# Splat attention in a graph kernel: distances in five fp32r passes, scores over all 128 rows, normalisation per head, and transposes moved to the seams of groups

## What is computed

```python
qkv = (x @ qkv_w.T).reshape(b, t, 3, h, hd)
q, k, v = (qkv[:, :, 0], qkv[:, :, 1], qkv[:, :, 2])
centers = base_centers + center_deltas * ms
def splat_weights(tok):
    d2 = jnp.sum(tok ** 2, -1)[..., None] + c_sq[None, None] - 2.0 * jnp.einsum('bthd,hsd->bths', tok, centers)
    return jnp.exp(-d2 * inv_var[None, None]) * eff_amps[None, None]
qw = splat_weights(q)
kw = splat_weights(k)
logits = jnp.einsum('bihs,bjhs->bijh', qw, kw) / temp
attn = jax.nn.softmax(logits, axis=2)
out = jnp.einsum('bijh,bjhd->bihd', attn, v).reshape(b, t, d)
return out @ out_w.T
```

## Time and profile before

| | before |
|---|---|
| median of three executions | 940.78 us |
| the profiled execution, its own time | 937.67 us |
| its span, first to last instruction | 935.9 us |
| PE, DVE, ACT, POOL busy | 818.8, 602.2, 309.2, 61.4 us |
| chain that ended last, by engine | PE 17%, DVE 5%, ACT 1%, issue 1% of the span |

### The profile page before, as it was taken

The page is one execution under the profiler, slowest core; times in us unless marked ns, Lnnn a source line. Parts: engine busy times, 40 slices in busy tenths (PEclk is TensorE's granted clock), DMA queues, the critical chain, the costliest instruction groups (busy, mean ns, idle before and its releaser), DMA issues. The chain is left out here.

```text
span 935.9 us, 11276 instructions
## 1 busy us (share of the span) xinstructions
PE 818.8 (87%) x3978; PEld 563.4 (60%) x3978; DVE 602.2 (64%) x1180; ACT 309.2 (33%) x484; POOL 61.4 (7%) x60
## 2 busy tenths in 40 slices
PE   5788999999999960996769999988887999999788
PEld 3576788888778840332557778544454445546564
DVE  7646777776649553113882323688877888885876
ACT  2232334332214230112121103322313787884240
POOL 3000000000000004011280000000000000000010
PEclk9979999999999995999579999999998999999999
DMA  5814122210302415995320202000000100000002
GB/s 168 231 49 154 49 88 69 68 58 8 113 0 90 137 69 161 290 361 175 90 80 0 90 1 91 0 1 2 1 1 5 43 1 1 1 1 1 6 1 90
DMA packets 48150, 66.62 MB, mean 71 GB/s; under 512 B 4268, under 2 KB 22460, under 8 KB 48095
## 3 DMA queue, kind: packets, MB, share of 16 engines
q1 hardware_dynamic: 43903, 56.22, 18.8%
q0 software_dynamic: 2384, 6.92, 2.3%
q10 hardware_dynamic: 1808, 2.75, 0.8%
HBM read 56.38 MB, written 9.50 MB: 70 GB/s over the span
## 5 line engine op out<-in xcount | busy, mean ns | idle before, releaser
L851 PE MATMUL bank<-xT,slot 128*128 128x512 f32 (+1 forms) x248 | 105.3, 425 | 6.5 <-DVE xT L1564 5.7
L851 PE MATMUL bank<-slot 128*128 128x512 f32 (+1 forms) x212 | 87.7, 414 | 13.9 <-DVE slot L1566 8.3
L852 PE MATMUL bank<-xT,slot 128*128 128x512 f32 (+1 forms) x248 | 97.8, 394 | 0.0
L853 PE MATMUL bank<-xT,slot 128*128 128x512 f32 (+1 forms) x248 | 97.5, 393 | 0.0
L1314 ACT ACTIVATE slot<-bank 128x512 fp32r<-128x512 f32 (+3 forms) x60 | 33.9, 589 | 155.4 <-PE bank L1093 67.1
L2041 DVE TENSOR_REDUCE key<-bank 128x2 f32<-128x1024 f32 x64 | 75.3, 1218 | 14.8 <-PE bank L1153 14.8
L852 PE MATMUL bank<-slot 128*128 128x512 f32 (+1 forms) x212 | 84.2, 397 | 0.0
L853 PE MATMUL bank<-slot 128*128 128x512 f32 (+1 forms) x212 | 84.0, 396 | 0.0
L1501 ACT ACTIVATE arena<-bank 128x1024 f32<-128x1024 f32 x64 | 65.6, 1027 | 27.5 <-PE bank L1219 27.4
L851 PEld LDWEIGHTS bank<-xT,slot 128*128 128x128 f32 (+1 forms) x248 | 46.7, 188 | 22.5 <-issue 13.5
L1081 PE MATMUL bank<-arena,wraw 128*80 128x512 f32 x128 | 59.4, 609 | 0.0
(11 more groups left out here) (308 smaller groups left out, 1519.4 us busy)
## 6 DMA issues: line engine op xcount, KB each, us to landing
arena<-in_ewT SPq DMA_DIRECT2D x16, 1024.0 KB, 8.5
arena<-in_edge_attr SPq DMA_DIRECT2D x16, 512.0 KB, 3.9
wraw<-in_qkvT SPq DMA_DIRECT2D x3, 1024.0 KB, 5.2
expert_rows<-rows SPq DMA_DIRECT2D x1, 2560.0 KB, 13.6
wraw<-in_L_ffn_expert_b POOLq DMA_DIRECT2D x16, 160.0 KB, 5.8
expert_results<-wraw ACTq DMA_DIRECT2D x16, 160.0 KB, 5.7
xn<-in_x SPq DMA_DIRECT2D x4, 512.0 KB, 6.0
wraw<-in_L_mix_w_qkv SPq DMA_DIRECT2D x2, 1024.0 KB, 7.8
```

Source lines behind the costliest of these rows:

```text
L851: pe.matmul(out, L[1], R[0], start=start, stop=False, **kw)
L852: pe.matmul(out, L[0], R[0], start=False, stop=False, **kw)
L853: return pe.matmul(out, L[0], R[1], start=False, stop=stop, **kw)
```

## The change

- **Distances.** ACT's copy and square of a `p` go to `raw_sq`; ACT rounds both to a high half in one instruction over 1024 columns, and POOL subtracts for the low half (`split_sq`, a ring of four). `d2` becomes five fp32r passes: ones with the high and low squares, and `mm3` with the centres, which DVE splits once, after `cblk`. ACT also takes over the scaling and rounding of the weights.
- **Scores.** The keys of a pair are laid out twice with zeros in the other head's rows: POOL copies rows 0 to 63 of the key stack to `lone_keys` (second half of `wraw`) and clears them in the stack. `E` then takes 128 rows in both matmuls. For the unused rows to be harmless their log amplitude becomes -100.
- **Attention.** `normalise_group` becomes `normalise_head`, one head behind unit place 2 and the other behind place 3. `oT(g)` moves from place 4 of group g+1 to the seam of group g+2, between `E` and the first `O` (g = 0 to 4; 5, 6 and 7 stay late).
- **Staging.** `F` goes to the first staging buffer, behind the split of `Lo`.

```diff
+        if n >= lag and (n - lag) % T == 0 and n >= lag + 2 * T and (n - lag) // T - 2 != 2 * PAIRS - 3:
+            steps.append(("oT", (n - lag) // T - 2))
         if n >= lag:
             steps.append(("O", n - lag))
...
         if group > 0 and place == 2:
             steps.append(("oU", group - 1))
-        if group > 0 and place == 4 and group - 1 != 2 * PAIRS - 3:
+        if group > 0 and place == 3:
+            steps.append(("oN", group - 1))
+        if group == 2 * PAIRS - 1 and place == 4:
             steps.append(("oT", group - 1))
...
+            for i in range(4 * PAIRS):
+                pool.wait_ge(sq_hi, i + 1)
+                pool.tensor_tensor(split_sq[:, i % 4, 1], raw_sq[:, i % 4], f32(split_sq[:, i % 4, 0]), ALU.subtract).then_inc(sq_lo, 1)
+
+            pool.wait_ge(w_split, windex["Lv"] + 1)
+            pool.wait_ge(sq_lo, 4 * PAIRS)
+            pool.memset(f32(lone_keys)[64:128], 0.0).then_inc(keys_zeroed, 1)
+            pool.wait_ge(keys_zeroed, 1)
+            for c in range(PAIRS):
+                finished(pool, "L", c, T - 1, 1)
+                if c >= 2:
+                    finished(pool, "E", 2 * T * (c - 1) - 1)
+                both = slot[3][0:64, c // 2, 2 * (c % 2):2 * (c % 2) + 2, :].rearrange("p a i -> p (a i)")
+                pool.tensor_copy(lone_keys[0:64, c % 2, :], both.bitcast(F32)).then_inc(keys_copied, 1)
+                pool.wait_ge(keys_copied, c + 1)
+                pool.memset(both.bitcast(F32), 0.0).then_inc(keys_alone, 1)
...
-                    pe.matmul(o, onesblk, qsq[:, g % 2, 1, w], start=True, stop=False)
-                    close(pe.matmul(o, cblk[:, c, :], qsq[:, g % 2, 0, w], start=False, stop=True))
+                    pe.matmul(o, onesblk[:, :], split_sq[:, i % 4, 0, 1], start=True, stop=False)
+                    pe.matmul(o, onesblk[:, :], split_sq[:, i % 4, 1, 1], start=False, stop=False)
+                    close(mm3(o, [at_[:, c, :] for at_ in centers], [split_sq[:, i % 4, v, 0] for v in range(2)], False, True))
...
-                        r = krows(b, MROWS)
-                        ins = pe.matmul(bank[:, bank_of[step] + b, :], stack(3, c, r, jt * P, (jt + 1) * P),
-                                        stack(2, c, r, ih * HALF, (ih + 1) * HALF), start=True, stop=True)
+                    pe.wait_ge(keys_alone, c + 1)
+                    w, every = slice(jt * P, (jt + 1) * P), slice(0, P)
+                    for b, keys in enumerate((lone_keys[:, c % 2, w], stack(3, c, every, jt * P, (jt + 1) * P))):
+                        ins = pe.matmul(bank[:, bank_of[step] + b, :], keys,
+                                        stack(2, c, every, ih * HALF, (ih + 1) * HALF), start=True, stop=True)
...
+                    act.activation(raw_sq[:, i % 4, 0], at(*step), ACT.Copy)
+                    act.activation(raw_sq[:, i % 4, 1], at(*step), ACT.Square).then_inc(evicted[bank_of[step]], 1)
+                    emptied(act, *step)
+                    act.activation(split_sq[:, i % 4, 0], raw_sq[:, i % 4], ACT.Copy).then_inc(sq_hi, 1)
...
+                    emptied(act, *step)
+                    if side == "q":
+                        link(act.activation(w, w, ACT.Identity, scale=par[:, 6, c:c + 1]))
+                    act.activation(pring[:, i % 4, HALF:2 * HALF].bitcast(F32R), w, ACT.Copy).then_inc(wh_ready, 1)
...
-            dve.tensor_tensor(csquare, flat, flat, ALU.mult).then_inc(blk_ready, 1)
+            link(dve.tensor_tensor(csquare, flat, flat, ALU.mult))
+            link(dve.tensor_copy(centers[0][:, :, :], cblk))
+            dve.tensor_tensor(centers[1][:, :, :], cblk, f32(centers[0]), ALU.subtract).then_inc(blk_ready, 1)
...
-                emptied(dve, *step)
+                dve.wait_ge(wh_ready, i + 1)
-                if side == "q":
-                    link(dve.tensor_scalar(w, w, par[:, 6, c:c + 1], None, ALU.mult))
-                link(dve.tensor_copy(wh, w))
```

More of the change, by code:

```diff
@@ L320, in build @@
     for name, _, _ in WEIGHTS:
-        stage_of[name] = {"W1a": 2, "W2a": 3}.get(name, (loads[0] + loads[1]) % 2)
+        stage_of[name] = {"W1a": 2, "W2a": 3, "F": 0}.get(name, (loads[0] + loads[1]) % 2)
         place_of[name] = loads[stage_of[name]]
@@ L524, in build @@
         st_ready = sem("st_ready")
+        keys_zeroed = sem("lone_keys_zeroed")
+        keys_copied = sem("lone_keys_copied")
+        keys_alone = sem("keys_alone")
+        sq_hi = sem("squares_hi")
+        sq_lo = sem("squares_lo")
+        wh_ready = sem("weights_hi")
         mx_ready = sem("mx_ready")
@@ L539, in build, with side_number, side_step @@
         out_sent = sem("out_sent")
+        def side_number(step):
+            _, side, c, th = step
+            return 4 * c + 2 * "qk".index(side) + th
+        def side_step(kind, i):
+            return (kind, "qk"[i // 2 % 2], i // 4, i % 2)
         def finished(eng, *name):
@@ L1479, in _ @@
                         act.wait_ge(st_ready, i - 3)
-                    act.activation(pring[:, i % 4, 0:HALF], at(*step), ACT.Exp,
+                    w = pring[:, i % 4, 0:HALF]
+                    act.activation(w, at(*step), ACT.Exp,
                                    bias=par[:, 5, c:c + 1], scale=par[:, 4, c:c + 1]).then_inc(evicted[bank_of[step]], 1)
+                    emptied(act, *step)
+                    if side == "q":
+                        link(act.activation(w, w, ACT.Identity, scale=par[:, 6, c:c + 1]))
+                    act.activation(pring[:, i % 4, HALF:2 * HALF].bitcast(F32R), w, ACT.Copy).then_inc(wh_ready, 1)
                 elif step[0] == "V1":
@@ L2054, in _, with normalise_head @@
                     lo(step)
-            def normalise_group(g):
+            def normalise_head(g, b):
                 finished(dve, "oU", g)
                 c, ih = g // 2, g % 2
-                for b in range(2):
-                    o = bank[:, b, 0:TH * (HD + 1)].rearrange("p (t m) -> p t m", t=TH)
-                    r = c_a[:, b * TH:(b + 1) * TH]
-                    link(dve.reciprocal(r.unsqueeze(2), o[:, :, HD:HD + 1]))
-                    h = 2 * c + b
-                    ins = dve.tensor_tensor(xn[:, ih * TH:(ih + 1) * TH, h * HD:(h + 1) * HD], o[:, :, 0:HD],
-                                            r.unsqueeze(2).to_broadcast([P, TH, HD]), ALU.mult)
-                    if b == 0:
-                        link(ins)
-                ins.then_inc(evicted[0], 1)
-                emptied(dve, "oU", g)
-                dve.sem_inc(o_ready, 1)
+                o = bank[:, b, 0:TH * (HD + 1)].rearrange("p (t m) -> p t m", t=TH)
+                r = c_a[:, b * TH:(b + 1) * TH]
+                link(dve.reciprocal(r.unsqueeze(2), o[:, :, HD:HD + 1]))
+                h = 2 * c + b
+                ins = dve.tensor_tensor(xn[:, ih * TH:(ih + 1) * TH, h * HD:(h + 1) * HD], o[:, :, 0:HD],
+                                        r.unsqueeze(2).to_broadcast([P, TH, HD]), ALU.mult)
+                if b == 0:
+                    link(ins)
+                else:
+                    ins.then_inc(evicted[0], 1)
+                    emptied(dve, "oU", g)
+                    dve.sem_inc(o_ready, 1)
             def p_high(n):
@@ L2088, in _ @@
                     maxima(step)
-                elif step[0] == "oU":
-                    normalise_group(step[1])
+                elif step[0] in ("oU", "oN"):
+                    normalise_head(step[1], int(step[0] == "oN"))
                 elif step[0] == "oT":
```

35 lines of the change are left out of this document (19 added, 16 removed).

## The result

The change takes 936.76 us (median of seven runs, 934.43 to 938.49), the kernel before beside it 940.95 (seven runs, 939.15 to 941.94): a ratio of 0.9958, 95% interval 0.9943 to 0.9974. It is faster by 4.2 us, 10.7 were forecast. The time lies in the range, the sign is right, the size is not.

What follows compares the result with a forecast made beforehand. DVE's preparation was taken to bound the splat blocks, DVE the splat turns with scores, PE attention. +3.3 - 7.8 - 6.2 = -10.7 us took the profiled 937.67 to 927.0; the median's 3.1 more made 930.1, range 924 to 938.

Steps and rivals of the forecast that it cites:

- Part 1: Splat blocks: DVE's splitting of the centres, with waits for POOL's additions, delays the low half PE needs: +3.3 us.
- Weights: Splat turns with scores: DVE loses the scaling and rounding of q weights and rounding of k weights: -8.6 us.
- earlier start: Splat turns 1 to 3: five-pass distances end DVE's idling before the first reduction sooner, 0.2, 0.6 and 0.6: -1.4 us.
- Turn 0: First splat turn: ACT's chains replace PE's distances as the limit, so 0 us, ends -1 and +1.
- `Lv`, a coin flip: Turn 3: DVE's split of `Lv` may come just behind a POOL subtraction, half a chance of 2.6 us: +1.2.
- Key copies: POOL's key copies hold DVE: the first meet stackings, +1.0 us; those of pairs 2 and 3, inside attention, +2.0.
- Attention: Attention in sum: full-row scores, seams, normalisation stalls and key copies, -7.5 - 1.4 + 0.7 + 2.0 = -6.2 us.
- Full rows: Attention: 128-row scores shorten a unit from 1.96 to 1.84 us in some 60 of 64 PE-bound units: -7.5 us.
- the seams: Attention: moved transposes of results fill 0.29 us of PE waiting at each of five seams: -1.4 us.
- The fourth rival: TensorE's clock falls in the distances, where PE works less; three turns lose 2 us each: 936 us, chance 0.06.
- The first and second: Attention rivals: score gap is semaphore waits, 937.6 us, chance 0.08; full-row scores lose overlap and keep gap, 950.6, chance 0.04.
- the third: Splat turns: POOL's subtractions meet DVE's stackings and split, 937.9 us, chance 0.12; far end, reductions held too, 948, 0.01 of it.

Runs made afterwards that it cites:

- e1: The changed kernel with DVE splitting the centres behind the second quarter of `H` instead of ahead of the first low half: 931.27 us, ratio 0.9889.
- e7: The changed kernel with distances as two plain fp32 matmuls on unsplit squares and the centres not split: 932.93 us, ratio 0.9927.
- e2: The changed kernel with POOL waiting for the split of `Lv` before one subtraction of squares in the last pair: 933.32 us, ratio 0.9913.
- e8: The changed kernel with 50-row scores, both heads normalised at once and all result transposes at place 4; POOL's key copies stay: 939.99 us.
- e5: The changed kernel with both heads normalised in one piece behind unit place 2: 935.48 us.
- e9: The changed kernel with PE waiting for the normalisation's own semaphore instead of a signal DVE sends after waiting for itself: 933.15 us, ratio 0.9927.
- e4: The changed kernel with scores over 50 rows, both heads at once as before, key copies left in: 938.92 us.
- e6: The changed kernel with the transposes of results back at place 4 of the next group, normalisation still in halves: 939.37 us.

## Why the prediction was right in direction and wrong in size

- **Part 1, +3.3**: +3.0 in the account, +2.7 to +3.1 in the profiles that differ by it. Right, by the assumed mechanism. Not foreseen was that this term need not be paid at all (e1).
- **Weights, -8.6, and earlier start, -1.4**: turns 1 and 2 gave 3.2 and 3.4 of the 3.1 and 3.5 forecast. Right in sum; e7 shows the earlier start at 0.3 and 0.5 us, not 0.2 and 0.6. Turn 0 cost 0.6 instead of 0, inside the ends given.
- **`Lv`, a coin flip of +1.2**: this is the first step that failed. It was named, but with half a chance of 2.6 us; it cost 2.7 (e2) and fell on the bad side in all ten profiles without the remedy (4.32 or 4.33 us each time), so it was set by the order of work and not by chance. Even with it undone, turn 3 gains 2.3 and not 3.5; the granted clock fell there too, and the rest was not separated.
- **Key copies, +1.0 and +2.0**: 0 in turn 4, and nothing visible in the change's attention, where the groups with a copy take 16.1 us like the others. The mechanism is real, though, only smaller and hidden there behind DVE's wait for itself: each copy costs 0.4 us in e8, 0.7 to 0.8 in e5, and 0.2 in e9.
- **Attention, -6.2**: -6.0, but by errors that cancel. Full rows were given -7.5 (60 units at -0.12 are in fact -7.2); e4 shows -3.9. This step failed too, and by the most. The passes do keep 0.23 us, but nearly each unit was taken as bound by PE, and in a group of eight three save little or nothing: the one behind DVE's wait for itself (2.04 to 2.11 us), the seam, which waits for ACT (2.40 to 2.42), and the unit before the place of the old transposes (1.93 to 1.96 instead of 1.97). The 0.7 us for new stalls was too small for that. What offset it is mainly the key copies, 2.0 forecast and not visible; the seams gave the 1.4 they were given (e4 against c1).
- **The tail, not in the sum**: +3.0 with what lies ahead of it. Here a term was put at nothing without a reason. The fourth rival had put a fall of TensorE's clock into the distances; it came in turn 3, behind PE's wait for DVE, and in the tail, over 200 us behind the last distance. A stretch that the change does not touch was taken as fixed. The split of the profiles behind e9 makes 2.3 of the 3.0 look like bad luck of timing, since e5, e6 and e9 do without it; that is not shown.
- **The level**: the forecast was set on the profiled 937.67 plus 3.1, and the median of before stayed at 940.3 to 941.4; that step held.
- **Rivals.** The first and second are refuted by the even 0.23 us. Of the third the `Lv` collision came true, and in small the key copies; reductions were not held. That agrees with the Trainium skill, "SBUF — State Buffer", section "Who interferes with whom": a reduction does not contend, two SBUF inputs do. The same section of the Trainium skill calls the shared ports an exclusive lock and says that the order of issue decides who blocks, and the trace agrees: POOL's subtraction, 0.20 us ahead, kept its 2.38 us and the split waited for it; the one that came 1.17 us before the split's end took 3.38 instead.

The 5.1 us between -10.7 and -5.6 are thus: turns 1 to 4, 1.6 (2.7 lost in turn 3, 1.0 got back from the copies); turn 0, 0.6; behind attention, 3.0; attention 0.2; less 0.3 at part 1. That attention stands there with 0.2 is luck: two errors of 3.6 and 2.0 us and smaller ones met.

## What to carry to other kernels

An engine's new work beside another's is not a cost times a chance: write down for each collision which of the two starts first, and if the loser is on the path, let the other wait; POOL idled 4 us in e2 and the kernel gained 3.4. A saving per unit counts only in the units that this engine bounds: count the others first. When PE idles a few us between dense stretches, look at what comes behind: if its clock falls where another engine sets the pace it is free, if it falls in passes on the path it costs their length again. With attention 0.6 us shorter (e9) or 2.0 longer (e5) the one became the other here, so compare stretches and not totals before such 2 us are put down to an edit. Judge a part by undoing all that belongs to it at once (e8), since undoing one piece can make a wait that neither kernel has (e6).

## What the runs showed of the hardware

- Full-row passes of fp32r kept 0.23 us between starts at the clock's higher level, scores and `O` alike; two 50-row matmuls at once took 0.44 us, with 0.09 more before and 0.05 more behind them.
- TensorE's lower level (passes 0.43 us apart) came in the tail at one of two places: for 3.4 us with the first idling, of 2.76 us, in nine profiles, or, 15 us later, for 6.8 us behind one of 3.3 to 3.5 us, in seven. The first idling is the same in all sixteen, and what decides between the places stays open.
- A rounding copy of 128x512 on DVE, one SBUF operand, was held by POOL's reading (1.37 us beside an addition and 1.23 beside a copy instead of 0.42), a reduction from PSUM was not (2.34 for two).
- A DVE queue that waits for its own last instruction before it signals stood still 0.23 us; without that, attention was 0.6 us shorter with no computation changed.
